# Windowed attention with routing on one core: values gathered by two indirect DMAs a region that GpSimd begins, in place of SyncE's four gathers

## What is computed

```python
x_n = group_norm(x)                                  # per image, 32 groups of 8 channels
q, k, v = split(x_n @ qkv_w.T + qkv_b)               # 256 channels each
idx = top_k(region_mean(q) @ region_mean(k).T, 4)    # 4 of 49 regions for each region
keys, vals = k[regions idx], v[regions idx]          # 4 x 64 = 256 rows for each region
out = softmax((q * 256**-0.5) @ keys.T) @ vals       # 8 heads of 32
out = out + depthwise_conv_3x3(v) + conv_b           # taps over neighbouring cells of v
result = x + out @ out_w.T + out_b
```

## Time and profile before

| | |
|---|---|
| median of 3 runs | 1902.72 us (1897.96 to 1905.69) |
| profiled execution: its own time | 1898.2 us |
| profiled execution: span of the trace | 1896.3 us |
| busy share: TensorE, VectorE, ScalarE, GpSimd | 91%, 82%, 81%, 43% |
| chain that ended last | SyncE's queue 77% |

### The profile page before, as it was taken

How to read it: one execution, slowest core, us unless ns; L and a number is a source line. 1 busy time by engine, 2 the same in 40 slices (tenths; PEclk the granted TensorE clock), 3 DMA queues, 4 the chain that set the end, 5 groups by cost and what they waited for, 6 DMA issues and landing times.

```text
span 1896.3 us, 73094 instructions
## 1 busy us (share of the span) xinstructions
PE 1725.6 (91%) x24776; PEld 1055.4 (56%) x24776; DVE 1545.8 (82%) x3427; ACT 1538.4 (81%) x4905; POOL 810.5 (43%) x2256
## 2 busy tenths in 40 slices
PE   4969999999999999999999999999999999978776
PEld 2535555655665655555555555665565656544443
DVE  5878989888987888888888889888888888876443
ACT  1548988888987888888888889888888898867774
POOL 1124444444454444444444444544444444444332
PEclk9989999999999999999999999999999999999999
DMA  3223333343443343344333334434343333333232
GB/s 123 80 60 101 121 121 120 116 119 120 120 125 107 121 120 122 116 121 119 122 119 114 118 121 122 133 101 122 119 121 97 110 109 104 110 98 99 87 101 85
DMA packets 157006, 211.47 MB, mean 112 GB/s; under 512 B 17888, under 2 KB 144736, under 8 KB 156640
## 3 DMA queue, kind: packets, MB, share of 16 engines
q1 hardware_dynamic: 141408, 129.71, 23.8%
q0 software_dynamic: 15232, 77.08, 12.2%
HBM read 155.33 MB, written 51.38 MB: 109 GB/s over the span
## 4 chain that ended last, share of the span: by engine, by line
SPq 77%; issue 12%; DVE 5%; PE 3%; DMA 2%; ACT 1%; POOL 0%; POOLq 0%; DVEq 0%; ACTq 0%
SPq L234 58%; SPq L209 17%; DVE lepe L514 3%; SPq L224 2%; DMA v_dram<-v_stage 2%; PE chunk_bank L735 1%; DVE stats L531 1%; DVE x_sum L540 1%; PE chunk_bank L746 1%; PE s_bank L735 0%; DMA v_sel<-v_dram 0%; DMA xn<-x_dram 0%; DVE neg_max L610 0%; SPq L241 0%; PE s_bank L803 0%
## 5 line engine op out<-in xcount | busy, mean ns | idle before, releaser
L425 ACT ACTIVATE probs<-s_bank,neg_max 128x256 f32<-128x256 f32 x1568 | 735.2, 478 | 201.3 <-DVE neg_max L610 201.3
L284 POOL COPY k_sel<-k_all 128x128 f32 x1568 | 400.9, 299 | 684.9 <-PE s_bank L803 681.8
L514 DVE SCALAR_TENSOR_TENSOR lepe<-v_band,taps,lepe 128x448 f32<-128x448 f32 x896 | 612.8, 714 | 68.1 <-POOL v_band L310 54.8
L610 DVE TENSOR_REDUCE neg_max<-s_bank 128x2 f32<-128x512 f32 x784 | 506.0, 685 | 117.6 <-PE s_bank L803 114.9
L735 PE MATMUL chunk_bank<-xn,wqkv 128*128 128x448 f32 x1248 | 549.7, 549 | 3.7 <-DVE xn L550 3.5
L432 ACT COPY probs_t<-pt_bank 128x512 f32<-128x512 f32 x784 | 469.3, 599 | 53.2 <-PE pt_bank L816 51.9
L816 PE MATMUL pt_bank<-ident,probs 128*128 128x128 f32 x3136 | 492.2, 280 | 13.7 <-ACT probs_t L432 12.3
L816 PEld LDWEIGHTS pt_bank<-ident,probs 128*128 128x128 f32 x3136 | 360.9, 141 | 189.4 <-issue 120.6
L295 POOL TENSOR_TENSOR lepe<-o_norm,lepe 128x128 f32<-128x128 f32 x392 | 282.6, 721 | 261.1 <-DVE o_norm L628 260.9
L425 ACT ACTIVATION_READ_ACCUMULATOR probs<-s_bank,neg_max 128x1 f32 x1568 | 322.2, 206 | 0.0
L830 PEld LDWEIGHTS o_bank<-probs_t,v_sel 128*32 128x32 f32 x12544 | 194.5, 110 | 219.5 <-DMA v_sel<-v_dram 156.6
(11 more groups left out here) (68 smaller groups left out, 1114.2 us busy)
## 6 DMA issues: line engine op xcount, KB each, us to landing
v_sel<-v_dram SPq DMA_DIRECT2D x1568, 64.0 KB
xn<-x_dram POOLq DMA_DIRECT2D x56, 448.0 KB, 4.4
v_dram<-v_stage SPq DMA_DIRECT2D x112, 224.0 KB
resid<-x_dram POOLq DMA_DIRECT2D x56, 448.0 KB, 4.0
out_dram<-resid POOLq DMA_DIRECT2D x56, 448.0 KB
wqkv<-w_qkv_dram SPq DMA_DIRECT2D x1, 768.0 KB, 10.2
wout<-w_out_dram SPq DMA_DIRECT2D x1, 256.0 KB, 12.4
idx_row<-top_idx SPq DMA_DIRECT2D x8, 0.8 KB
```

What stands on the lines that cost most here:

```text
L284: last = pool.tensor_copy(k_sel[:, r % K_SLOTS, :, RT * j:RT * (j + 1)], k_all[:, b % 2, :, bass.ds(reg[j] * RT, RT)])
L425: act.activation(probs[:, u, :], s_bank[:, u, 0:KEYS], ACT.Exp, bias=neg_max[:, r % 2, u:u + 1], accum_out=denom[:, r % 2, u:u + 1]).then_ ...
L514: ins = dve.scalar_tensor_tensor(row, v_band[:, n % BANDS, k, t // 3:t // 3 + RS, t % 3:t % 3 + W], taps[:, k, t:t + 1], row, ALU.mult, AL ...
L610: dve.tensor_reduce(neg_max[:, r % 2, 2 * hf:2 * hf + 2], s_bank[:, 2 * hf:2 * hf + 2, 0:KEYS], AX.X, ALU.max, negate=True).then_inc(max_d ...
```

## The change

SyncE gathers no values any more. In their place GpSimd's `select_values` begins two indirect DMAs a region: each fills 128 partitions, one for each half of the 256 rows, and takes the row number for every partition from a tensor `v_idx` in SBUF. The row numbers are made once an image: VectorE spreads the chosen region numbers over 64 columns each (`spread_rows`), TensorE turns that into one column a region by two matmuls with the identity (`value_rows`), and VectorE multiplies by 8 and adds each partition's own offset (`v_idx_out`). The wait for the slot (`attn_done`) is the same, but stands on GpSimd; so does the wait for the stored values, once an image. `v_dram` is split into two tensors.

```diff
 # GpSimd
+            def select_values(r):
+                b = r // NREG
+                if r % NREG == 0:
+                    pool.wait_ge(v_idx_done, b + 1)
+                    pool.wait_ge(v_stored, 32 * NWIN * (b + 1))
+                if r >= V_SLOTS:
+                    pool.wait_ge(attn_done, r - V_SLOTS + 1)
+                for c in range(CH):
+                    pool.indirect_dma_start(
+                        v_sel[:, r % V_SLOTS, c, :], None, v_flat[b % 2],
+                        bass.IndirectOffsetOnAxis(ap=v_idx[:, b % 2, c, r % NREG:r % NREG + 1], axis=0)
+                    ).then_inc(v_sel_in[r % V_SLOTS], 16)
...
                     if is_region(r + 2):
                         gather_keys(r + 2)
+                    if is_region(r + 2) and (r + 2) % NREG >= 2:
+                        select_values(r + 2)
+                    elif is_region(r + 2) and (r + 2) % NREG == 1:
+                        select_values(r + 1)
+                        select_values(r + 2)
                     if is_region(r - 2):
                         take_region(r - 2)
...
 # SyncE
-                    if is_region(r + 2) and (r + 2) % NREG >= 2:
-                        select_values(r + 2)
                     if rc == 6 and rr == LAST and is_row(s + A_LEAD):
-                        n = s + A_LEAD
-                        store_values(n)
-                        sp.wait_ge(idx_in, 16 * (n // NWIN + 1))
-                        sp.wait_ge(v_stored, 32 * (n + 1))
-                        select_values(r + 1)
-                        select_values(r + 2)
+                        store_values(s + A_LEAD)
...
 # VectorE, steps 3 and 4 of an image's first row
+            def spread_rows(b):
+                dve.wait_ge(top_done, b + 1)
+                if b:
+                    dve.wait_ge(v_idx_full, b)
+                dve.tensor_copy(chosen_rows[:].rearrange("p c (h t) -> p (c h) t", h=2),
+                                top_idx[:, 0:TOPK].unsqueeze(2).to_broadcast([NREG, TOPK, RT])).then_inc(rows_spread, 1)
+
+            def v_idx_out(b):
+                dve.wait_ge(v_idx_full, b + 1)
+                if b >= 2:
+                    dve.wait_ge(attn_done, NREG * (b - 1))
+                dve.tensor_scalar(v_idx[:, b % 2, :, :].rearrange("p c r -> p (c r)"), side(0, CH * NREG), float(RS),
+                                  v_base[:, 0:1], ALU.mult, ALU.add).then_inc(v_idx_done, 1)
...
 # TensorE, step 4 of an image's first row
+            def value_rows(b):
+                pe.wait_ge(rows_spread, b + 1)
+                for c in range(CH):
+                    last = pe.matmul(side(NREG * c, NREG), chosen_rows[:, c, :], ident[0:NREG, 0:NREG], start=True,
+                                     stop=True)
+                last.then_inc(v_idx_full, 1)
...
             def attend(r):
-                pe.wait_ge(v_sel_in[r % V_SLOTS], 16 * TOPK * (r // V_SLOTS + 1))
+                pe.wait_ge(v_sel_in[r % V_SLOTS], 16 * CH * (r // V_SLOTS + 1))
```

More of the change, by code:

```diff
@@ L67, in chunk_places, with attention_kernel @@
     return places, used
-def attention_kernel(nc, x, w_qkv, w_out, b_qkv, b_out, w_tap, b_tap, ident_d, group_d, v_dram, out):
+def attention_kernel(nc, x, w_qkv, w_out, b_qkv, b_out, w_tap, b_tap, ident_d, group_d, base_d, v_dram, out):
+    v_flat = [kept.rearrange("q t c -> (q t) c") for kept in v_dram]
     place, chunks_in = chunk_places()
@@ L125, in attention_kernel @@
         idx_row = sb("idx_row", [1, 2, TOPK * NREG], U32)
+        chosen_rows = sb("chosen_rows", [NREG, CH, P])
+        v_base = sb("v_base", [P, 1])
+        v_idx = sb("v_idx", [P, 2, CH, NREG], U32)
         s_bank = ctx.enter_context(nc.psum_tensor("s_bank", [P, HG, 512], F32))
@@ L152, in attention_kernel @@
         sums_ready, means_evac, top_done = map(sem, ("sums_ready", "means_evac", "top_done"))
+        rows_spread, v_idx_full, v_idx_done = map(sem, ("rows_spread", "v_idx_full", "v_idx_done"))
         halo_done, lepe_step, lepe_rows = sem("halo_done"), sem("lepe_step"), sem("lepe_rows")
@@ L203, in is_region @@
             return 0 <= r < ALL
-        N_WEIGHTS = 7
+        N_WEIGHTS = 8
         def chosen(engine, r):
@@ L223, in store_values @@
                 for h in range(2):
-                    sp.dma_start(v_dram[b % 2, h:RS:2, rr * W:(rr + 1) * W, :].rearrange("q t d -> t q d"),
+                    sp.dma_start(v_dram[b % 2][h:RS:2, rr * W:(rr + 1) * W, :].rearrange("q t d -> t q d"),
                                  v_stage[PADW * h:PADW * h + W, :, :]).then_inc(v_stored, 16)
[L227 to L235, removed]
             def load_index(b):
@@ L250, in _ @@
             sp.dma_start(bout[:], b_out).then_inc(weights_in, 16)
+            sp.dma_start(v_base[:], base_d).then_inc(weights_in, 16)
             for s in rows_in_order():
@@ L678, in _ @@
                         affinity_out(ar // NWIN)
+                    elif rc == 4 and begins_a:
+                        v_idx_out(ar // NWIN)
                     elif rc == 2 and ends_x:
@@ L711, in _ @@
                     elif rc == 3:
+                        if begins_a:
+                            spread_rows(ar // NWIN)
                         outer_tap(now, 11)
@@ L865, in _ @@
                         pe.wait_ge(aff_taken, ar // NWIN + 1)
+                    elif rc == 4 and first and is_row(ar):
+                        value_rows(ar // NWIN)
+                    elif rc == 5 and first and is_row(ar):
+                        pe.wait_ge(v_idx_done, ar // NWIN + 1)
                     elif rc == 2 and last_row and is_row(xr):
@@ L932 @@
         "group": np.kron(np.eye(P // GROUP), np.full((GROUP, GROUP), 1.0 / GROUP)).astype(np.float32),
+        "base": (np.arange(P) % RT // RS * (NREG * RS) + np.arange(P) % RS)[:, None].astype(np.float32),
     }
@@ L935 @@
     args = [nc.dram_tensor(f"{n}_dram", list(a.shape), F32, kind="ExternalInput").ap() for n, a in arrays.items()]
-    v_dram = nc.dram_tensor("v_dram", [2, RS, NREG * RS, C], F32, kind="Internal").ap()
+    v_dram = [nc.dram_tensor(f"v_dram{i}", [RS, NREG * RS, C], F32, kind="Internal").ap() for i in range(2)]
     out = nc.dram_tensor("out_dram", [ROWS, P, KC, ROW], F32, kind="ExternalOutput").ap()
```

## The result

The changed kernel takes 2296.82 us, the median of four runs, against 1901.53 us before: 1.207 times as long, with a 95% interval of 1.204 to 1.211. The forecast was 2150 us in a range of 2065 to 2420. The profiled execution took 2292.7 us, with a span of 2290.9.

A forecast was written before the change was run, and what follows sets the result against it. SyncE (4.2 us a region) and TensorE (4.3) were taken as bounds. 1898 us plus 186 for the halo loop, 54 for image borders and 5 for row numbers gave 2143, adjusted to 2148, say 2150; range 2065 to 2420.

The forecast's parts named there:

- SyncE's part: SyncE loses its 1568 gathers and 392 register loads and stops being a bound; worth at most 58 us.
- The order on GpSimd: At a row's end, slot wait and two indirect DMAs stand ahead of addition and halo, delaying VectorE's first tap.
- The size of d: Time of one indirect DMA on GpSimd, taken as 1.0 us, the middle of 0.556 and 1.46.
- the halo loop: Path through GpSimd, VectorE, ScalarE and TensorE around the halo: 7.19 + 2d us, making 35.3 us a row against 31.5.
- E to E': From the end of step 6's attention matmuls on TensorE to the next ones' end: 4.00 us before, 7.19 + 2d after.
- step 6: Last of a row's steps, numbered 0 to 6; its indirect DMAs wait for its own attention matmuls, ahead of the halo.
- the dear rival: Indirect DMA at d = 1.46, GpSimd the bound at 40.3 us a row; lower clock likewise: 2400 us, chance 0.20.
- GpSimd's own loop: GpSimd's work of 14.6 + 14d us a row plus 5.35 us of waiting: 19.9 + 14d us a row.
- Images' borders: Last row of each image: GpSimd waits for stored values and starts four DMAs; 6.7 us, eight times, 54 us.
- the cheap DMA: Indirect DMA on GpSimd costs what a plain one does, d = 0.556: 2095 us, chance 0.18.
- the single fetch: Each index of GpSimd's indirect DMA is fetched on its own, d = 10 us: some 9,000 us, chance 0.04.
- the faster one: Halo isn't late for VectorE's taps, the wait hides and the 58 us gain remains: 1845 us, chance 0.08.

The follow-up runs named there:

- e6: Changed kernel with halo copies in step 5, and SyncE gathering two of each region's four by plain DMAs, GpSimd two by one indirect DMA: 1868.22 us, 0.981 of before.
- e11: e6 with the row's three plain DMAs (x, result, residual) started by SyncE instead of GpSimd: 1865.13 us, 0.978 of before.
- e1: Changed kernel with the halo copies moved from step 6 to step 5, ahead of that step's slot wait and indirect DMAs: 2042.28 us, 1.072 of before.
- e2: Changed kernel with slot wait and two indirect DMAs moved to the end of GpSimd's step, behind addition and halo: 2062.25 us, 1.084 of before.
- e3: Kernel before plus one GpSimd wait per step for the attention matmuls, behind the key copies, without indirect DMAs: 2059.33 us, 1.081 of before.
- e9: Kernel before with the halo copies moved to GpSimd's step 5, behind the key copies: 1902.08 us, 0.999 of before.
- e10: Changed kernel, halo still in step 6, with the row's three plain DMAs started by SyncE instead of GpSimd: 2264.33 us, 1.188 of before.
- e5: Changed kernel with each indirect DMA filling 64 partitions instead of 128: 2291.82 us, 1.202 of before.

## Why the prediction was right, point by point

- **SyncE's part** was right: it left the chain, TensorE's wait for values vanished. e6 and e11, which take half of the gathers from SyncE and let GpSimd bound nothing, show a gain of 36 to 39 us, under the bound of 58. In the last image I had counted nothing; its 49 regions, from the end of the image before to its own end, took 213.2 us and now take 201.9, 11 us less, since some steps there hung on SyncE after all: before, TensorE's weight loads waited for gathered values at 20 places there, 21.2 us in all.
- **The order on GpSimd** was right in its place and its mechanism; e1, e2 and e3 show it by moving the halo, by moving the DMAs, and by the wait alone. One premise was wrong: that a row with a halo has no slack there before the change. In e9 most of the 54.8 us of waits went and the time stayed.
- **The size of d** was right: 1.021 us against 1.0. I had it as a choice between two bounds; no run shows why an indirect DMA costs 0.47 us more than a plain one of 128 pieces, so the closeness is partly luck.
- **The step that fell short is the sum of the halo loop**, 7.19 + 2d = 9.2 us for E to E', where 11.69 was measured. By terms, medians over 36 such steps of the trace against the prediction's: E to the first DMA 1.21 against 0.25; the two DMAs 2.29 against 2.0; the addition and halo 0.93 against 0.84; taps to spread 1.86 against 1.63; spread to the next scores 3.23 against 3.20; scores and attention 2.17 against 1.27. So three things were left out: GpSimd comes late into step 6 (0.96), which e10 takes away; a gap of 0.30 us between two indirect DMAs; and TensorE's low clock behind the wait (0.90), which I had only in the dear rival. Smaller, the taps beside the key copies took 0.23 more. A row came out 2.4 us longer than the 35.3 forecast, 49 x 2.4 = 118 us.
- **GpSimd's own loop** was sized too small as well. I had 14.6 + 14d = 28.9 us of work a row at the measured d; e1, where GpSimd is the bound, shows 33.9. Of the 5.0, 7 x 0.46 = 3.2 are the idle 0.16 and 0.30 us in front of the DMAs. Most of the rest is the slowing of its copies beside VectorE's taps: in e1's 30 rows they took 10.3 us a row against my 7.1, while the additions took 3.3 against 5.0.
- **Images' borders**: the last halo step of an image takes 18.5 us, 6.8 more than the others (medians), where I had 6.7. GpSimd stands there until the stored values have landed, which the profile can't name, and then starts four DMAs, here with E at 1230.5:

```profile
1235.31 1.02 POOL L285 DMA_INDIRECT v_sel<-v_dram,v_idx  x1 [5.03 <-issue]
...
1239.16 0.95 POOL L285 DMA_INDIRECT v_sel<-v_dram,v_idx  x1 [0.31 <-issue]
```

  But the two rows at a border take about 88 us instead of 2 x 37.7, 13 more. The other 6 lie in the steps around it, for which I had no term: above all the first step of the next image, 6.0 to 6.8 us against 3.95, with the matmuls of the region means and more of the low clock. 8 x 6.3 = 50 us.

With these the sum closes to 7 us: 2143 + 118 + 50 - 11 = 2300 us against the 2292.7 us of the profiled run.

The time lies in the range, but just above the 2110 to 2280 us to which I gave half of the chance. The range went so high for the sake of a dear DMA, which did not come; that lateness, gaps and clock filled the same place is luck.

Of the rivals, the cheap DMA and the single fetch fell with the measured d and e5, the faster one with VectorE's 7.0 us a row. The dear one has a right half: the clock falls already at d = 1, in all 36 halo steps compared (scores 1.15 to 1.16 us).

## What to carry to other kernels

Before work with a wait is put on an in-order queue, list what is queued behind it and who waits for that: here one wait cost 154 us without any of the work (e3), and in the changed kernel two small copies moved ahead of it gave back 255 (e1). When an engine takes over DMAs, count for each the idle time in front of it too, and what its other operations lose beside a busy neighbour. Where two engines can both start a kind of transfer, sharing it may beat giving all of it to either (e6: 1868 us against 1902 and 2297).

## What the runs showed of the hardware that was not expected

- An indirect DMA on GpSimd costs nearly the same for 64 and for 128 rows (0.945 and 1.021 us). In the changed kernel each is preceded by at least 0.30 us of idle time behind another one, or 0.16 us behind another operation, that no wait explains. The Trainium skill (DMA: Bandwidth & Descriptors, Latency and other measured facts) puts a DMA that GpSimd starts at about 1 us to its first byte. That is a latency, and the rows here are time on the engine that starts the DMA (1.02 us for an indirect one, 0.56 for a plain one, 0.617 on SyncE), so no run here shows it; the prediction was wrong to see agreement in SyncE's row.
- GpSimd's operations slow down beside VectorE's taps: four key copies took 1.00 us alone and 1.78 us beside them. In the whole trace of the changed kernel a copy mostly beside a tap took 0.75 us at the median (116 copies), with VectorE idle 0.31 (262), and beside the maxima 0.29 (761). The taps slow down too: two took 1.53 us instead of 1.28. So what a queue costs depends on what it meets.
- TensorE's clock fell to its lower level in the halo step of ordinary rows, where it waited 5.86 us, but also in e3, where the longest of the waits in that step was 2.27 us and the scores took 1.16 us. How long it stays low varies: e10 shortened the wait, and the clock came back later.
